# The third attention's maxima split by GpSimd in place of VectorE, under another planned order

## The reference

```python
logits = jnp.einsum('bhqd,bhkd->bhqk', q, k) / jnp.sqrt(jnp.asarray(dh, q.dtype))
neg = (1.0 - mask.astype(q.dtype)) * -1000000000.0
logits = logits + neg[:, None, :, :]
attn = jax.nn.softmax(logits, axis=-1)
attn = attn * group_prob[:, None, :, :]
out = jnp.einsum('bhqk,bhkd->bhqd', attn, v)
```

## Time and profile before

| | us |
|---|---|
| median of three runs | 1506.46 |
| profiled execution | 1494.83 |
| its span, first to last instruction | 1493.0 |
| TensorE busy | 1369.8 (92%) |
| VectorE busy | 1085.1 (73%) |
| ScalarE busy | 795.1 (53%) |
| GpSimd busy | 156.6 (10%) |
| mean granted TensorE clock | 0.969 |

### The profile page before, as it was taken

One profiled execution on the slowest core, in us unless ns is written; L12 is line 12 of the kernel. 1 busy time (PEld: TensorE's weight loads), 2 busy tenths in 40 slices (PEclk: granted clock), 3 DMA queues, 4 the chain that ended last, 5 costly groups with the idle time before them and its releaser, 6 DMA issues. The chain is left out here.

```text
span 1493.0 us, 29555 instructions
## 1 busy us (share of the span) xinstructions
PE 1369.8 (92%) x9483; PEld 763.5 (51%) x9519; DVE 1085.1 (73%) x2623; ACT 795.1 (53%) x1507; POOL 156.6 (10%) x185
## 2 busy tenths in 40 slices
PE   6878989999999999999999999999999989889990
PEld 3556566664454544443353343343545445578990
DVE  5786744457664777789999999998868877563325
ACT  5375755536647666665455465555666545323332
POOL 1101011100100100001010000000000003224223
PEclk8799999999999999999999999999999989999996
DMA  6223323301402542434343333122222231676754
GB/s 230 79 68 102 104 48 86 86 26 27 127 23 80 163 122 52 137 94 121 104 143 98 93 123 86 51 65 53 62 53 56 52 105 57 206 292 194 213 182 179
DMA packets 124482, 158.32 MB, mean 106 GB/s; under 512 B 31372, under 2 KB 103820, under 8 KB 122348
## 3 DMA queue, kind: packets, MB, share of 16 engines
q1 hardware_dynamic: 120930, 147.06, 33.9%
q0 software_dynamic: 3408, 9.38, 1.7%
HBM read 66.38 MB, written 29.44 MB: 64 GB/s over the span
## 5 line engine op out<-in xcount | busy, mean ns | idle before, releaser
L1668 ACT ACTIVATE prob<-ps 128x512 f32<-128x512 f32 (+3 forms) x832 | 404.0, 550 | 202.8 <-PE ps L1441 108.1
L1960 DVE TENSOR_REDUCE mx<-ps 128x1 f32<-128x512 f32 (+3 forms) x512 | 281.3, 585 | 80.3 <-PE ps L1409 42.4
L1441 PE MATMUL ps<-of_expert 99*128 99x512 bf16 (+4 forms) x768 | 252.4, 357 | 8.2 <-DMA of_expert<-mrow 3.3
L1441 PEld LDWEIGHTS ps<-of_expert 99*128 99x128 bf16 (+1 forms) x768 | 73.1, 98 | 95.5 <-ACT prob L1668 35.7
L1476 PE MATMUL ps<-prob,va 128*32 128x512 f32 (+3 forms) x1024 | 117.0, 530 | 0.2
L1407 PE MATMUL ps<-of_expert 120*128 120x512 bf16 x256 | 92.0, 380 | 3.6 <-DVE mx L1960 0.4
L1401 PE MATMUL ps<-of_expert 96*128 96x512 bf16 x256 | 86.7, 381 | 6.2 <-DVE mx L1956 5.3
L1956 DVE CUSTOM_DVE_ANT_0 ps<-ps,room_a 128x512 f32<-128x512 f32 x128 | 86.1, 710 | 5.5 <-PE ps L1401 5.2
L1956 DVE CUSTOM_DVE_ANT_0 ps<-ps,room_b 128x512 f32<-128x512 f32 x128 | 85.9, 708 | 1.7 <-PE ps L1401 1.4
L1398 PE MATMUL ps<-of_expert 96*128 96x128 bf16 (+3 forms) x256 | 72.4, 306 | 9.0 <-DVE mx L1960 7.3
L1658 ACT ACTIVATE mrow<-ps 12x512 bf16<-12x512 bf16 x64 | 37.2, 581 | 77.3 <-PE ps L1423 77.2
(11 more groups left out here) (251 smaller groups left out, 2550.4 us busy)
## 6 DMA issues: line engine op xcount, KB each, us to landing
of_expert<-parts SPq DMA_DIRECT2D x384, 128.0 KB, 2.4
sorted<-zeros SPq DMA_DIRECT2D x27, 650.0 KB, 7.7
room_a<-in_w SPq DMA_DIRECT2D x30, 512.0 KB, 4.1
otc<-oraw SPq DMA_DIRECT2D x256, 32.0 KB, 2.0
room_b<-in_w SPq DMA_DIRECT2D x15, 512.0 KB, 4.2
ct<-in_c SPq DMA_DIRECT2D x8, 512.0 KB, 3.8
of_expert<-in_w SPq DMA_DIRECT2D x8, 512.0 KB, 8.2
wa<-in_attention SPq DMA_DIRECT2D x4, 768.0 KB, 5.0
```

The costliest lines, as they stand in the source:

```text
L1441: i = pe.matmul(dst[:, lo:S], ks[0:rows, h, t], qs[0:rows, h, lo:S], start=(a != MASKED), stop=(a != CAUSAL and not fixed))
L1668: act.activation(prob[:, quad % PROBS, n, lo:S], key_bank(*st)[:, lo:S], ACT.Exp).then_inc(s_exp, 1)
L1960: i = dve.tensor_reduce(mx[:, slot, s, n:n + 1], src[:, 0:width], AX.X, ALU.max)
```

## The change

In MASKED alone, step P is executed by GpSimd, by five instructions; the other attentions keep their four on VectorE. GpSimd gets a remainder buffer of its own and a semaphore of its own for "split". VectorE waits for GpSimd's split of four groups earlier before it takes the first maximum of a group (the slot of `mx` is read by GpSimd, no longer by VectorE itself). The planner charges the step 1.5 us on GpSimd. The whole table LAG has other numbers, and so the order of all engines is another one.

```diff
+def splits_maxima(u):
+
+    return "POOL" if kind_of(u) == MASKED else "DVE"
...
-            room += [(("P", i // G, i % G), "DVE")] if i >= 0 else []
+            room += [(("P", i // G, i % G), splits_maxima(i // G))] if i >= 0 else []
...
-        return [("DVE", 0.8, [(("S", u, g, quads(u) - 1, J - 1), "DVE")] + ([(("M", i // G, i % G), "PE")] if i >= 0 else []))]
+        return [(splits_maxima(u), 0.8 if splits_maxima(u) == "DVE" else 1.5, [(("S", u, g, quads(u) - 1, J - 1), "DVE")] + ([(("M", i // G, i % G), "PE")] if i >= 0 else []))]
...
-        return [("PE", 0.25, room + [(("P", u, g), "DVE")]), ("ACT", 0.6, [(("M", i // G, i % G), "SP")] if i >= 0 else []),
+        return [("PE", 0.25, room + [(("P", u, g), splits_maxima(u))]), ("ACT", 0.6, [(("M", i // G, i % G), "SP")] if i >= 0 else []),
...
-LAG = {"IN": -3.7, "CA": 26.5, ("CA", 1): 25.9, "FS": 13.8, "OP": -5.3, ("OP", 0): 1.6, ("OP", 1): -4.0, ("OP", 3): 2.1, "M":
-       -0.3, ("M", 1): 0.4, ("M", 2): -0.9, "C": -14.7, ("C", 0): -1.6, ("V", 1): 0.2, ("C", 1): -4.5, ("V", 2): -0.2, ("C", 3):
...
-       1): 4.6, ("E", 1): 7.0, ("EI", 1): 5.0, ("CL", 3): 47.4, "EA": 0.9, ("E", 3): -8.6, ("EU", 0): -1.2, ("EX", 2): -33.3,
-       ("OU", 3): 0.1, ("ED", 2): 5.6, "MN": 0.9, ("C", 2): 9.2, ("SX", 2): 2.0, ("CG", 2): 1.3, ("CL", 1): 2.9, "RC": -21.6,
...
+LAG = {"CA": 0.8, ("CA", 1): 0.3, "FS": -10.1, "OP": -5.5, ("OP", 0): 2.5, ("OP", 1): -3.1, ("OP", 3): -10.2, "M": -0.3, ("M", 1):
+       0.4, ("M", 2): -0.7, "C": -17.7, ("C", 0): -1.2, ("V", 1): 0.2, ("C", 1): 0.7, ("V", 2): -0.2, ("C", 3): 2.0, "R": -0.8,
...
+       4.0, "ED": 3.9, ("ED", 0): -15.6, ("EH", 1): 0.9, ("EU", 1): 1.4, ("E", 1): 14.6, ("EI", 1): 13.6, ("E", 3): -2.4, ("EU",
+       0): -1.3, ("EX", 2): -8.7, ("ED", 2): 25.6, "MN": 0.5, ("C", 2): 14.6, ("SX", 2): -3.4, ("CG", 2): -9.4, "RC": -20.5, "RK":
...
-        mr = sb("mr", [P, NT, J])
+        mr = [sb(f"mr{i}", [P, NT, J]) for i in range(2)]
...
-                        pe.wait_ge(s_mp, nth("P", u, g))
+                        pe.wait_ge(*split_ready(u, g))
...
+                elif kind == "P" and splits_maxima(st[1]) == "POOL":
+                    u, g = st[1:]
+                    slot = (G * u + g) % MAXIMA
+                    m, p3 = mx[:, slot, :, :], mp[:, slot, :, :, :]
+                    before = G * u + g - MAXIMA
+                    pool.wait_ge(s_max, nth("S", u, g, quads(u) - 1, J - 1))
+                    pool.wait_ge(s_mt, nth("M", before // G, before % G))
+                    pool.tensor_scalar(p3[:, :, 0, :], m, -1.0, None, ALU.mult).then_inc(s_g, mine.one())
+                    pool.tensor_scalar(mr[1][:, :, :], m, -1.0, None, ALU.mult).then_inc(s_g, mine.one())
+                    pool.wait_ge(s_g, mine.count)
+                    pool.tensor_tensor(mr[1][:, :, :], mr[1][:, :, :], p3[:, :, 0, :], ALU.subtract).then_inc(s_g, mine.one())
+                    pool.wait_ge(s_g, mine.count)
+                    pool.tensor_copy(p3[:, :, 1, :], mr[1][:, :, :]).then_inc(s_g, mine.one())
+                    pool.wait_ge(s_g, mine.count)
+                    pool.tensor_tensor(p3[:, :, 2, :], mr[1][:, :, :], p3[:, :, 1, :], ALU.subtract).then_inc(s_mg, 1)
...
+                    before = G * u + g - MAXIMA
+                    if s == 0 and n == 0 and before >= 0 and splits_maxima(before // G) == "POOL":
+                        dve.wait_ge(*split_ready(before // G, before % G))
...
-                elif kind == "P":
+                elif kind == "P" and splits_maxima(st[1]) == "DVE":
```

More of the change, by code:

```diff
@@ L1038, in decoder @@
         s_mp = sem("maximum_split")
+        s_mg = sem("masked_maximum_split")
         s_mt = sem("maximum_turned")
@@ L1078, in decoder, with split_ready @@
         DOWN = {st[1:3]: i + 1 for i, st in enumerate(x for x in ORDER if x[0] == "DN" and x[3] == 3)}
+        def split_ready(u, g):
+            mine = [st[1:] for st in ORDER if st[0] == "P" and splits_maxima(st[1]) == splits_maxima(u)]
+            return s_mg if splits_maxima(u) == "POOL" else s_mp, mine.index((u, g)) + 1
         def op_ready(u, g, o):
@@ L1971, in _ @@
                     dve.wait_ge(s_v, mine.count)
-                    dve.scalar_tensor_tensor(mr[:, :, :], m, -1.0, p3[:, :, 0, :], ALU.mult, ALU.subtract).then_inc(s_v, mine.one())
+                    dve.scalar_tensor_tensor(mr[0][:, :, :], m, -1.0, p3[:, :, 0, :], ALU.mult, ALU.subtract).then_inc(s_v, mine.one())
                     dve.wait_ge(s_v, mine.count)
-                    dve.tensor_copy(p3[:, :, 1, :], mr[:, :, :]).then_inc(s_v, mine.one())
+                    dve.tensor_copy(p3[:, :, 1, :], mr[0][:, :, :]).then_inc(s_v, mine.one())
                     dve.wait_ge(s_v, mine.count)
-                    dve.tensor_tensor(p3[:, :, 2, :], mr[:, :, :], p3[:, :, 1, :], ALU.subtract).then_inc(s_mp, 1)
+                    dve.tensor_tensor(p3[:, :, 2, :], mr[0][:, :, :], p3[:, :, 1, :], ALU.subtract).then_inc(s_mp, 1)
                 elif kind == "E":
```

## The result

The changed kernel takes 1520.4 us (median of four runs, 1516.99 to 1523.26) against 1505.87 us (four runs of the kernel before on the same chip): a ratio of 1.0101, 95% interval 1.0079 to 1.0123. It is slower by 1.0%, 15 us, where 9 us less were forecast.

The account below looks back on a forecast made before the run. VectorE was taken to pace the third attention, TensorE about a tenth behind. Terms -14.7 + 1 + 0.8 + 3 + 1 = -8.9, taken as -9 us, gave 1497.5 us against 1506.5; the gain's range was about 1486 to 1502.

Parts of the forecast that it names:

- Removed from VectorE, 14.7 us: Third attention: 16 splits leave VectorE, each costing it 0.92 us, nearly all on the path.
- GpSimd's split, 1.45 us free, 2.3 to 2.5 us held: Third attention: time of GpSimd's five instructions, undisturbed or held by a VectorE product; bounds 1.45 and 3.9 us.
- GpSimd holding products: Third attention: VectorE's products lose 1 us in all to GpSimd's split; as a rival 8 us, 1504.5 us, chance 0.04.
- The lateness at the transposes, 8 us with 3 us charged: Third attention: late splits hold TensorE at the transposes 8 us in all, bounds 0 and 38; 3 us charged.
- TensorE's spare 42 us takes part: Third attention: TensorE has some 42 us to spare, which absorbs part of the 8 us of lateness.
- The coupling, 1 us: Third attention: two nearly full engines in fixed-order queues waiting on two score banks lose 1 us, between 0 and 11.
- The order, nothing: All queues: the replaced table of lags is charged nothing; the range carries 6 us to either side.
- DMAs and queues behind: After the transposes: the copy, its DMA and SP's queue move along with the lateness; nothing charged.
- held splits: Rival, third attention's transposes: every split meets two products, 2.4 us late; +13 us, 1519.5 us, chance 0.10.
- the order costs: Rival, 1350 to 1493 us: another order lets TensorE's clock fall to 0.75; 20 us more there, 1517.5 us, chance 0.06.
- Given back: Rival, third attention: late splits, half absorbed by TensorE, return most of the gain; -2 us, 1504.5 us, chance 0.16.
- three signs of being wrong: Transpose wait past 20 us; products averaging 1.3 us or more; third attention's gain lost before 635 us or after its end.

Follow-up runs that it names:

- The runs with hardly any lateness: Kernel before, its order, third attention's split cut to one part of three: on GpSimd 0.9944, on VectorE 0.9949.
- the new order: The changed kernel's order: GpSimd splitting (changed kernel) 1.0101, VectorE splitting 1.0045, GpSimd with transposes later 1.0093, GpSimd with one part 1.0011.
- the old order: Order of the kernel before, with GpSimd doing the third attention's split: full split 1.0157, two parts 1.0038, one part 0.9944.
- one part for three: Kernel before, its order, VectorE doing only the split's first instruction in the third attention, other two parts zero: 0.9949.
- Without fills: Kernel before without the filling matmuls in the third attention: 1.0023.
- the old order, transposes later: Kernel before's order with GpSimd's split, each masked transpose moved behind next steps worth 1.2 us of TensorE: 1512.32 us, 1.0057.

## Why the prediction was wrong

**The bound** was read rightly as far as it was tested: 8.0 us less work on VectorE, with the split a little earlier, shorten the third attention by 7.4 us.

**Removed from VectorE, 14.7 us.** Too much, but not the fault that decides. Busy time fell by 10.4 us, near the 11 expected, although two products grew by 2.3 us. The runs with hardly any lateness show what relief is worth: 6.0 and 7.4 us. The time between a split and its neighbours on VectorE was counted as gained; how much of it was gained was not measured by itself.

**GpSimd's split, 1.45 us free, 2.3 to 2.5 us held.** Right in the main: 1.35 us from its first instruction to its last when free (0.14 us after the maximum), 2.2 to 2.4 us held once, 3.1 to 3.3 held twice. 10 of 16 were held by at least most of a product, the "bit over half" expected. The Trainium skill's page SBUF — State Buffer (section Who interferes with whom) says that a VectorE instruction with two SBUF inputs contends with a GpSimd instruction that reads SBUF, for a port pair that one of them holds alone; the rows agree, 1.10 to 1.31 us in place of 0.25. The other direction, GpSimd holding products, was priced at 1 us. For the split's short instructions it was not seen: the products averaged 1.216 us with them and 1.217 without, in the same order. For GpSimd's bias additions it was: 3.03 and 1.76 us in place of 1.22. The prediction looked for this only in the splits, and the new order brought it in by another step.

**The lateness at the transposes, 8 us with 3 us charged: the step that failed.** The wait was 13.3 us, just above the 5 to 12 us named, so its size was nearly right. What failed is "TensorE's spare 42 us takes part". The spare time is a sum over the attention (and too large a one: from 635 to 1010 us TensorE was busy 362.9 of 375 us, 19.5 of it with fills, which leaves some 32); a late split is late at one place, and the scores queued behind it are what VectorE works on next, with two banks between them. VectorE's wait for scores grew from 6.6 to 16.1 us. None of the lateness was seen to be absorbed: with the order the same, VectorE's idle time grew by 13.6 us for 13.3 us of wait (10.9 of them before unit 12's first maximum), and in the old order the attention grew by 11.9 us for 12.1. That two banks are too few to cover it is read from the timeline of one split; the number of banks was not varied. The term should have been the whole wait, 11 to 13 us in place of 3, which with a relief of 6 to 7 us alone turns the sign.

**The coupling, 1 us.** VectorE's idle time grew by 15.4 us. Most of it is this same wait and no term of its own: 9.5 us more in waits for scores against before. Its waits for ScalarE's parts, for projections and for a weight load grew too, from 6.6 to 15.5 us, but the new order has 11.3 us of these with VectorE splitting as well.

**The order, nothing.** It cost 0.45%, 7 us at the median, just beyond the 6 us left to either side. In the profiles the third attention is 1.6 us longer by it and the rest 2.3 us; the two held products would alone make up the first. Where the remainder goes is open: the stretches before unit 8 and behind unit 15 differ by more than that between executions (before unit 8 from 630.7 to 636.8 us among the four kernels with the new order, which run the same there).

**DMAs and queues behind.** Rightly nothing: on the page the turned scores waited 1.3 us for the rows of maxima in the whole run, 3.3 before.

```profile
L1453 PE MATMUL ps<-of_expert 99*128 99x512 bf16 (+4 forms) x768 | 252.4, 357 | 4.5 <-DMA of_expert<-mrow 1.3
```

Of the rivals it was "held splits" that came true in its place and mechanism, with less lateness than the 38 us it named and no absorption, and "the order costs" with its sign but in another place. That the first of them named 1519.5 us, close to the 1520.4 measured, is luck: 7 us of the loss are the order's. "Given back" was wrong for the same reason as the forecast. Of the three signs of being wrong none came: the wait stayed under 20 us, the products under 1.3 us on average, and the third attention gained nothing that the rest could lose. What told was the expected shortening by 8 to 10 us, which came out as 4.9 us more, with VectorE busy 92% of it in place of over 94. The Trainium skill's page Perfetto Trace Analysis (section Optimizing Scalar/DVE Operations) warns that moving work between VectorE and GpSimd over their shared port might not help; the runs agree: in the same order the move cost 0.56%, or 1.6% in the old one. They add where it is lost, in the time until the result is there, part of which is the holding by products.

Together: 7 us for the order and 8 for the split in it make the 15 us measured. The profiles of the new order with VectorE and with GpSimd have the 8 as 10.2 us less work and 13.6 us more idle time of VectorE in the third attention, and 5.5 us more in the rest, which go with the clock and whose cause is open.

## What to carry to other kernels

When a small chain of dependent instructions is moved to an idle engine, cost the time from its input to its result, not only the busy time it frees: where a third engine's in-order queue waits on the result, and the relieved engine lives on what stands behind in that queue, each microsecond of lateness came back in full here. TensorE's spare time, summed over the attention, absorbed nothing at a place where two banks lie ahead of its consumer. Moving the wait to a later place in the queue was no sure cure: it helped in one order and not in the other. Making the chain shorter (here one part for three, 0.9949) relieved the full engine and the waiting one at once, and needed no new order.

## What the runs showed that was not expected

The holding works both ways: a bias addition on GpSimd, work that was there before the change, made one product of VectorE last 3.03 us in place of 1.22 as soon as another order put the two beside each other. Without fills and with 17 us of TensorE at half clock, the attention that VectorE paces became only 2.7 us longer. And one GpSimd split took 5.3 us after its maximum, with four of five 128 x 16 instructions held, because four products in two pairs ran on VectorE meanwhile (the old order, transposes later):

```profile
1010.46 1.31 POOL L1818 TENSOR_SCALAR mp<-mx 128x16 bf16<-128x16 f32 x1 [14.38 <-DVE mx L2011]
1011.75 1.15 POOL L1819 TENSOR_SCALAR mr<-mx 128x16 f32<-128x16 f32 x1
1012.98 0.23 POOL L1821 TENSOR_TENSOR mr<-mr,mp 128x16 f32<-128x16 f32 x1
1013.28 1.20 POOL L1823 CAST mp<-mr 128x16 bf16<-128x16 f32 x1
1014.55 1.08 POOL L1825 TENSOR_TENSOR mp<-mr,mp 128x16 bf16<-128x16 f32 x1
```
